# Relative-position attention: the score band moved in 64-row pieces, one band buffer for each tile, and the output stored tile by tile

## Chip, cores and metric

The kernel runs on one core of a Trainium2 chip. The metric is the device time of one execution in microseconds (us), the median of several runs. The engines are named as in the profile: PE (TensorE matmul) and PEld (its weight loads), DVE (VectorE), ACT (ScalarE), POOL (GpSimd) and SP (SyncE, which here only issues transfers). SPq and POOLq stand for the issuing side of SP and POOL.

## What is computed

The program is a two-layer network over 16 sequences of 256 positions with 128 features. Each layer normalises its input and adds an attention part and a mixture-of-experts part to the residual. The change lies in the attention of the second layer, which has 16 heads of 8 features and a learned vector for each clipped distance:

```
idx = jnp.arange(s)
dist = jnp.clip(idx[None, :] - idx[:, None], -R, R) + R      # R = 64
pe_k = rel_emb_k[dist]
pe_v = rel_emb_v[dist]
score = jnp.einsum('bhqd,bhkd->bhqk', q, k) + jnp.einsum('bhqd,qkd->bhqk', q, pe_k)
attn = jax.nn.softmax(score, axis=-1)
ctx = jnp.einsum('bhqk,bhkd->bhqd', attn, v) + jnp.einsum('bhqk,qkd->bhqd', attn, pe_v)
```

The second score term depends on key minus query, clipped at 64 to either side. A tile of 128 queries needs it on a band that runs along the diagonal; outside the band it is constant in a row, and the kernel subtracts that constant, so that the term is zero there.

## The kernel before

The stages follow one another in blocks, at whose end all engines meet: a first stage (normalisation and the first mixture), the first attention, the second mixture, the second attention (`attn1_stage`) and a last block that stores the output (`store_stage`, one transfer of 2 MB).

The second attention takes 32 tiles of 128 queries, two for each of 16 sequences. An even tile holds the first 128 queries of its sequence (`it` 0), an odd tile the last (`it` 1). Each engine has its own written-out order, `step(r, i)`, for tile `s = 4r + i`. A tile has 8 pairs of heads (`hp`), in four quarters of two pairs (`q`). While tile `s` is scored, the band of tile `s + 1` is made and moved, and the weighted values of tile `s - 1` are finished:

- PE multiplies queries by the distance table into `ps_R` (`rel_scores`, L1407) for tile `s + 1`. ACT copies that into `Rt` (`keep_R`, L1542).
- SP sends a quarter of `Rt` to DRAM (`send_band`, L1741), into rows of `PITCH` pairs of values, and reads it back with a row stride that is one pair shorter (`fetch_band`, L1750). So each row is moved by one more position than the row above, and what was indexed by distance is indexed by key. Beside the band the DRAM rows hold zeros, written in an earlier stage (`clear_dram`).
- DVE adds the fetched band `Sb` to the key scores and takes the row maximum (`add_scores`, L1609). ACT takes the exponentials, PE transposes them, and so on.

`Rt`, `Sb` and the two DRAM buffers `skew` are shared as follows: `skew` has one buffer for even and one for odd tiles; `Rt` and `Sb` are single. `Sb` is 320 keys wide, of which the band takes 192 and DVE clears 64 on either side once. Tile parity chooses which 256 of the 320 are read (`bias_of`).

The stacked operands of the next sequence (`stk`) also come by way of DRAM. POOL splits the projected queries and keys into three bf16 parts; SP writes the parts (`send_parts`, L1259) in an odd tile, reads nine query pieces in the next even tile (`stack_queries`, L1268, three in each of `fill(0)`, `fill(1)`, `fill(2)`) and three key pieces in the odd tile (`stack_keys`, L1278). PE needs all nine query pieces before the first `rel_scores` of the odd tile that follows.

SP issues in program order, and a wait holds all that is behind it:

```
fill(0)
send_band(s + 1, nit, 0)
fetch_band(s, it, 3)
fill(1)
send_band(s + 1, nit, 1)
fetch_band(s + 1, nit, 0)
fill(2)
send_band(s + 1, nit, 2)
fetch_band(s + 1, nit, 1)
```

After that come, in odd tiles, `send_parts`, and in all tiles `send_band` of quarter 3 and `fetch_band` of quarter 2. A send waits until ACT has copied its quarter (`R_ready`). A fetch waits until the send of its own quarter has landed (`skew_out`). ACT's copy of a quarter, and DVE's adding of it, wait until the fetch has landed (`skew_in`).

At the end of a tile's work DVE adds the two expert rows to it (`combine`, L1639), which finishes its 128 rows of `x_all`. POOL gathers those rows.

Of the kernel before, what the change touches and what calls it, by code (L numbers as in the profile page):

```python
# [12 lines left out]
P = 128  # L13
B, T, D = 16, 256, 128
# [961 lines left out]


ZW = 16
ZP = SLOTS // P * ZW // (2 * (P - 1))
CLEARS = D // ZW + 2 * 8 // ZP  # L980


def clear_dram(sp, zeros, slots_dram, skew, zeroed):

    for z in range(D // ZW):
        sp.dma_start(slots_dram.rearrange("(p s) d -> p s d", p=P)[:, :, z * ZW:(z + 1) * ZW],
                     zeros[:, :, :]).then_inc(zeroed, 16)
    some = zeros[:, :, :].rearrange("p a b -> p (a b)")[:, 0:ZP * 2 * (P - 1)].rearrange("p (n c) -> p n c", n=ZP)
    for p in range(0, HP, ZP):

        sp.dma_start(skew[0][:, p:p + ZP, 2 * BAND:2 * PITCH], some).then_inc(zeroed, 16)
        sp.dma_start(skew[1][:, p:p + ZP, 0:2 * (P - 1)], some).then_inc(zeroed, 16)
# [192 lines left out]
REL = 64  # L1185
NREL = 2 * REL + 1
BAND = P + REL
PITCH = BAND + P - 1
GI = 16
GH1 = GI // 2  # L1190
PARTS = 3
# [10 lines left out]
class Attn1Front:  # L1202


    def __init__(self, m):
        self.w_in = m.sb("a1w_in", [P, 3, D])
        self.w_out = m.sb("a1w_out", [P, D])
        self.qkf = m.sb("a1qkf", [P, 2, T])
        self.low = m.sb("a1low", [P, 2, T])
        self.prt = m.sb("a1prt", [P, PARTS, 2, T], BF16)  # L1210
        self.stk = [m.sb(f"a1stk{i}", [KS, 2, H1, T], BF16) for i in range(2)]
        names = ("loaded xb_ready qk_done qk_ready split parts_out stacked0 stacked1 v_done v_ready R_done R_ready "
                 "stacked_k0 stacked_k1 S_done S_ready P_ready T_done Ta_ready Tv_ready X_done X_ready c_done cT_ready rrep_ready "
                 "rdT_done rdT_ready y_done y_added pool_step vec_step cleared ids_ready rows_in first_added combined").split()
# [104 lines left out]
def attn1_stage(nc, front, x_all, xnT_all, a, gates, slot_ids, ident, one, bias_q, bias_k, bias_v, rel_st, tabs, pick, fold):  # L1319

    skew, parts = a["skew"], a["parts"]
    S2 = 2 * B
    LAG = 2
    RING = 4
    with Pool(nc) as m:
# [2 lines left out]

        vx = m.sb("a1vx", [P, 2, 2, H1, QW])
        Rt = m.sb("a1Rt", [P, HP, BAND, 2])
        Sb = m.sb("a1Sb", [P, HP, 2 * REL + BAND, 2])
        Pm = m.sb("a1Pm", [P, 2 * RING, T])
        nmx = [m.sb(f"a1nmx{i}", [P, H1]) for i in range(2)]
        PT = [m.sb(f"a1PT{i}", [P, 2, H1, P]) for i in range(2)]
# [36 lines left out]

            return h % (2 * RING)

        def bias_of(it, hp, n):

            c0 = REL * (1 - it)
            return Sb[:, hp, c0:c0 + T, n]

        def tiles_behind(r, i):

# [2 lines left out]
        with nc.Block() as block:  # L1385
# [150 lines left out]
            def _(act):  # L1536
                def keep_R(s, hp):
                    act.wait_ge(sm["R_done"], s * HP + hp + 1)
                    if hp % PQ == 0:

                        act.wait_ge(skew_in[hp // PQ], s * 16)
# [43 lines left out]
            def _(v):  # L1585
# [12 lines left out]
                def add_scores(r, i, hp):  # L1598

                    s = r * 4 + i  # L1600
                    it, par = tile_of(i)
                    if hp % PQ == 0:
                        v.wait_ge(skew_in[hp // PQ], (s + 1) * 16)
                    v.wait_ge(sm["S_done"], s * HP + hp + 1)
                    v.wait_ge(sm["T_done"], up(s * HP + hp + 1 - RING))
                    nc.vector.memset(taker[:, hp:hp + 1], 0.0)
                    for n in range(2):
                        h = 2 * hp + n
                        nc.vector.tensor_tensor_reduce(out=Pm[:, place(h), :], in0=ps_S[hp % 2][:, n, :], in1=bias_of(it, hp, n),  # L1609
                                                       scale=-1.0, scalar=3.0e38, op0=ALU.add, op1=ALU.min,  # L1610
                                                       accum_out=nmx[it][:, h:h + 1]).then_inc(sm["S_ready"], 1)

# [84 lines left out]
            @block.gpsimd  # L1697
            def _(pool):
                def copy_x(n):

                    pool.wait_ge(sm["v_done"], n)
                    nc.gpsimd.tensor_copy(xb[:, :], xnT_all[:, bass.ds(n * T, T)]).then_inc(sm["xb_ready"], 1)

                def gather(s):

                    pool.wait_ge(sm["combined"], s)
                    nc.gpsimd.tensor_copy(ids[:, :, :], slot_ids[:, :, bass.ds(s, 1)]).then_inc(sm["ids_ready"], 1)
                    pool.wait_ge(sm["ids_ready"], s + 1)
# [24 lines left out]

            @block.sync
            def _(sp):
                def send_band(s, it, q):

                    ps = slice(q * PQ, (q + 1) * PQ)
                    sp.wait_ge(sm["R_ready"], s * HP + (q + 1) * PQ)
                    c0 = 0 if it == 0 else 2 * (P - 1)  # L1740
                    sp.dma_start(skew[it][:, ps, c0:c0 + 2 * BAND], Rt[:, ps, :, :].rearrange("p n c h -> p n (c h)")).then_inc(skew_out[q], 16)  # L1741

                def fetch_band(s, it, q):

                    ps = slice(q * PQ, (q + 1) * PQ)
                    sp.wait_ge(skew_out[q], (s + 1) * 16)
                    flat = skew[it].rearrange("i n c -> (i n c)")
                    sp.dma_start(Sb[:, ps, REL:REL + BAND, :].rearrange("p n c h -> p n (c h)"),  # L1750
                                 bass.AP(flat.tensor, flat.offset + 2 * (q * PQ * PITCH + P - 1),
                                         [[2 * (HP * PITCH - 1), P], [2 * PITCH, PQ], [1, 2 * BAND]])).then_inc(skew_in[q], 16)

                def step(r, i):
                    s = r * 4 + i
# [37 lines left out]
                sp.wait_ge(keys_in[0], (B // 2 + 1) * KSTACK)  # L1793
                sp.wait_ge(sm["parts_out"], (B + 2) * 16)
                for q in range(QUARTERS - 1):
                    sp.wait_ge(skew_in[q], (2 * B + 1) * 16)
                sp.wait_ge(skew_out[3], (2 * B + 1) * 16)


def store_stage(nc, x_all, out):  # L1800
    with Pool(nc) as m:
        stored = m.sem("stored")
        with nc.Block() as block:
            @block.sync
            def _(sp):
                sp.dma_start(out.rearrange("b (t p) d -> p (b t) d", p=P), x_all[:, :, :]).then_inc(stored, 16)
                sp.wait_ge(stored, 16)


def program(nc, a):  # L1810
    with Pool(nc) as m:
# [73 lines left out]
```

## Time and profile before

| what | value |
|---|---|
| median of 3 runs | 1679.4 us (1679.25 to 1684.8) |
| profiled execution, first to last instruction (span) | 1677.5 us |
| PE / PEld / DVE / ACT / POOL busy over the span | 93% / 74% / 54% / 44% / 18% |
| second attention and output store | from 1102 us to the end |
| share of the 16 DMA engines, 1200 to 1600 us | 0.89, at 245 GB/s |
| granted PE clock, 1200 to 1600 us | 1.00 of 2.4 GHz |

The span is the one time that the trace has for the profiled execution; it lies 1.9 us under the median of the runs. Busy shares over the whole span are averages over stages with different limits, so the rows below are taken from the second attention alone. In a timeline row the bracket at the end gives the time for which the engine was idle before it, and what ended that time.

### The profile page before, as it was taken

How to read it: one execution, taken by the hardware profiler on the slowest of the kernel's cores; microseconds unless marked ns; L12 is line 12 of the kernel's file. 1: busy time of each engine (PE TensorE's matmuls, PEld its weight loads, DVE VectorE, ACT ScalarE, POOL GpSimd, SP SyncE). 2: the span in 40 equal slices, each digit the busy share in tenths (PEclk: the TensorE clock that was granted, in tenths of full speed). 3: DMA queues.
4: the chain of work that ended last, by engine and by line, in shares of the span. 5: the costliest groups of instructions: out<-in, count | busy, mean ns of one | idle time of the engine just before them, and what ended most of it. 6: DMA issues, size and time to landing. Idle time of an engine off the chain costs nothing. (4 is left out here: it accounts for less than half of the span.)

```text
span 1677.5 us, 38807 instructions
## 1 busy us (share of the span) xinstructions
PE 1552.2 (93%) x14424; PEld 1233.4 (74%) x14424; DVE 904.4 (54%) x3193; ACT 732.4 (44%) x1975; POOL 299.0 (18%) x376
## 2 busy tenths in 40 slices
PE   6899999999999999999599999959999999999996
PEld 5668888888888888888365656537777777777764
DVE  5336545454545454545322222237877777777774
ACT  2322222222222222222223232258888888888873
POOL 2010201111111101010430000003323332333232
PEclk9999999999999999999699999979999999999998
DMA  4009400000000000000243232258889998899886
GB/s 118 0 8 86 105 8 7 8 8 6 6 6 5 7 5 7 3 10 4 85 114 114 77 112 85 72 166 245 250 241 251 237 250 235 246 246 254 236 235 173
DMA packets 234032, 181.50 MB, mean 108 GB/s; under 512 B 82703, under 2 KB 223913, under 8 KB 233888
## 3 DMA queue, kind: packets, MB, share of 16 engines
q1 hardware_dynamic: 228514, 167.17, 37.1%
q0 software_dynamic: 5376, 12.44, 2.7%
q8 instruction: 89, 1.46, 0.4%
q14 instruction: 53, 0.43, 0.1%
HBM read 103.63 MB, written 75.78 MB: 107 GB/s over the span
## 5 line engine op out<-in xcount | busy, mean ns | idle before, releaser
L1547 ACT ACTIVATE a1Pm<-a1Pm,a1nmx 128x256 f32<-128x256 f32 x512 | 255.5, 504 | 0.4 <-DVE a1nmx L1609 0.3
L1609 DVE CUSTOM_DVE_ANT_0 a1Pm<-a1ps_S,a1Sb 128x256 f32<-128x256 f32 x512 | 196.1, 421 | 77.2 <-issue 75.5
L768 DVE TENSOR_TENSOR a0AT<-a0ps_AM,mask 128x384 f32<-128x384 f32 x256 | 125.5, 551 | 192.5 <-PE a0ps_AM L588 192.1
L773 DVE TENSOR_TENSOR a0MT<-a0ps_AM,mask 128x384 f32<-128x384 f32 x256 | 138.4, 555 | 88.2 <-PE a0ps_AM L609 85.1
L1542 ACT ACTIVATE a1Rt<-a1ps_R 128x384 f32<-128x384 f32 x264 | 128.6, 487 | 106.7 <-PE a1ps_R L1407 96.9
L1162 DVE TENSOR_TENSOR f1hid<-f1ge,f1ps_b 128x512 f32<-128x512 f32 x80 | 55.0, 688 | 192.1 <-PE f1ps_b L1095 182.4
L1426 PE MATMUL a1ps_T<-ident,a1Pm 128*128 128x128 f32 x1024 | 155.9, 275 | 0.0
L607 PE MATMUL a0ps_AM<-a0AT 128*128 128x256 f32 x512 | 152.9, 380 | 0.0
L572 PE MATMUL a0ps_qk<-xnT_all,a0w_in 128*128 (+1 forms) x512 | 138.3, 393 | 2.0 <-PEq L151 1.3
L715 ACT ACTIVATE a0qk<-a0ps_qk 128x512 f32<-128x512 f32 x128 | 76.4, 597 | 119.3 <-PE a0ps_qk L572 119.3
L1407 PE MATMUL a1ps_R<-rel_st,a1stk 72*128 72x192 bf16 x528 | 90.0, 253 | 35.5 <-ACT a1Rt L1542 13.2
L719 ACT ACTIVATE a0v<-a0ps_v 128x512 f32<-128x512 f32 x64 | 38.2, 597 | 191.0 <-PE a0ps_v L598 187.0
L1426 PEld LDWEIGHTS a1ps_T<-ident,a1Pm 128*128 128x128 f32 x1024 | 115.0, 142 | 0.4 <-issue 0.2
L723 ACT ACTIVATE a0oT<-a0ps_o 128x512 f32<-128x512 f32 x64 | 38.2, 597 | 170.2 <-PE a0ps_o L621 170.2
L608 PEld LDWEIGHTS a0ps_AM<-a0AT 128*128 128x128 f32 x512 | 97.3, 190 | 13.2
L1105 PE MATMUL f1ps_o<-f1wo,f1hid 128*128 128x128 f32 x768 | 90.0, 277 | 15.4 <-DVE f1hid L1162 15.4
L572 PEld LDWEIGHTS a0ps_qk<-xnT_all,a0w_in 128*128 128x128 f32 x512 | 87.1, 190 | 19.9 <-issue 12.1
L1105 PEld LDWEIGHTS f1ps_o<-f1wo,f1hid 128*128 128x128 f32 x768 | 87.0, 192 | 19.7 <-DVE f1hid L1162 11.9
L1416 PE MATMUL a1ps_S<-a1stk 72*128 72x256 bf16 x512 | 101.4, 280 | 0.0
L1093 PE MATMUL f1ps_a<-f1xT,f1w 128*128 128x512 f32 x192 | 100.0, 603 | 0.7 <-issue 0.7
L1547 ACT ACTIVATION_READ_ACCUMULATOR a1Pm<-a1Pm,a1nmx 128x1 f32 x512 | 99.6, 195 | 0.0
L609 PE MATMUL a0ps_AM<-a0AT 128*128 128x128 f32 x512 | 99.0, 275 | 0.0
(246 smaller groups left out, 2991.0 us busy)
## 6 DMA issues: line engine op xcount, KB each, us to landing
skew<-a1Rt SPq DMA_DIRECT2D x132, 384.0 KB, 5.4
a1Sb<-skew SPq DMA_DIRECT2D x131, 384.0 KB, 7.0
a1stk<-parts SPq DMA_DIRECT2D x153, 64.0 KB
a1stk<-parts SPq DMA_DIRECT2D x51, 192.0 KB
parts<-a1prt SPq DMA_DIRECT2D x18, 384.0 KB
f1w<-in_L_ffn_w_kernel SPq DMA_DIRECT2D x16, 344.0 KB
f1w<-in_L_ffn_w_kernel SPq DMA_DIRECT2D x16, 320.0 KB
f1wo<-in_L_ffn_wo_kernel SPq DMA_DIRECT2D x16, 320.0 KB
```

The source lines that it names most:

```text
L572: ins = nc.tensor.matmul(ps_qk[:, i, :], w_in[:, i, p * P:(p + 1) * P], xnT_all[:, bass.ds(b * T, T)], start=True, stop=True)
L607: nc.tensor.matmul(M[:, 0:T], S[:, 0:P], S[:, 0:T], start=True, stop=True)
L609: nc.tensor.matmul(M[:, T:HB], S[:, T:HB], S[:, T:HB], start=False, stop=True).then_inc(M_done, 1)
L768: nc.vector.tensor_tensor(AT[i][h][:, :], ps_AM[i][h][:, 0:HB], mask[:, :], ALU.mult).then_inc(A_ready, 1)
L773: nc.vector.tensor_tensor(MT[i][h][:, :], ps_AM[i][h][:, 0:HB], mask[:, :], ALU.mult).then_inc(M_ready, 1)
L1093: nc.tensor.matmul(ps_a[u % 2][:, :], w[i][:, u * P:(u + 1) * P], xT[i][:, :], start=True, stop=True).then_inc(a_done, 1)
L1105: ins = nc.tensor.matmul(ps_o[i][:, s, :], hid[:, c, s * P:(s + 1) * P], wo[i][:, c, :], start=(c == 0), stop=(c == HC - 1))
L1416: ins = nc.tensor.matmul(ps_S[hp % 2][:, n, :], stk[par][:, 0, h, it * P:(it + 1) * P], stk[par][:, 1, h, :], start=True, stop=True)
L1426: ins = nc.tensor.transpose(ps_T[k % 2][:, n, jt, :], Pm[:, place(2 * k + n), jt * P:(jt + 1) * P], ident[:, :])
L1542: nc.scalar.activation(Rt[:, hp, :, :], ps_R[:, :, :].rearrange("p n c -> p c n"), ACT.Copy).then_inc(sm["R_ready"], 1)
L1547: nc.scalar.activation(Pm[:, place(h), :], Pm[:, place(h), :], ACT.Exp, bias=nmx[it][:, h:h + 1], scale=-1.0, accum_out=den[it][:, h:h + 1 ...
L1609: nc.vector.tensor_tensor_reduce(out=Pm[:, place(h), :], in0=ps_S[hp % 2][:, n, :], in1=bias_of(it, hp, n), scale=-1.0, scalar=3.0e38, op0 ...
```

## The change

- A quarter of the band is sent as two transfers of 64 rows, and fetched as two. Each half moves only the columns that its rows need: for one half of the tile 128 pairs of values a row, for the other 192; it was 192 for all 128 rows. So there are 16 band transfers for each tile where there were 8, and a send or fetch of a quarter moves 128 KB and 192 KB in place of 384 KB. The semaphores of a quarter count 32 where they counted 16.
- `PITCH` goes from 319 to 320 pairs, so that a DRAM row is 2560 bytes long, not 2552; a sent row starts at a multiple of 512 bytes. The zeros beside the band are one pair wider.
- `Sb` becomes two buffers, one for even and one for odd tiles, each 256 keys wide. The part of each that no fetch writes is cleared once: that of the even buffer by DVE, that of the odd buffer by POOL (two clears each, over 64 rows). DVE waits for POOL's clears before its first step; SP and POOL no longer wait for DVE's.
- `store_stage` is gone. SP stores tile `s - 3` (64 KB) in the step of tile `s`, after the fetch of quarter 3 and before `fill(1)`, once `combine` has finished that tile. The last three tiles are stored after the last step, in the same block.

```diff
-PITCH = BAND + P - 1
+PITCH = BAND + P
...
-        Sb = m.sb("a1Sb", [P, HP, 2 * REL + BAND, 2])
+        Sb = [m.sb(f"a1Sb{i}", [P, HP, T, 2]) for i in range(2)]
...
+        def band_of(it, half):
+            keys = slice(0, P + half * REL) if it == 0 else slice(REL + half * REL, T)
+            return slice(half * REL, (half + 1) * REL), keys
...
-                nc.vector.memset(Sb[:, :, 0:REL, :], 0.0)
-                nc.vector.memset(Sb[:, :, REL + BAND:2 * REL + BAND, :], 0.0).then_inc(sm["cleared"], 1)
+                for half in range(2):
+                    ins = nc.vector.memset(outside(0, half), 0.0)
+                ins.then_inc(sm["cleared"], 1)
                 v.wait_ge(sm["cleared"], 1)
+                v.wait_ge(sm["edge_cleared"], 2)
...
-                pool.wait_ge(sm["cleared"], 1)
+                for half in range(2):
+                    nc.gpsimd.memset(outside(1, half), 0.0).then_inc(sm["edge_cleared"], 1)
+                    pool.wait_ge(sm["edge_cleared"], half + 1)
...
+                def store(s):
+                    sp.wait_ge(sm["combined"], s + 1)
+                    sp.dma_start(out_tiles[:, s, :], x_all[:, s, :]).then_inc(sm["stored"], 16)
...
-                    sp.dma_start(skew[it][:, ps, c0:c0 + 2 * BAND], Rt[:, ps, :, :].rearrange("p n c h -> p n (c h)")).then_inc(skew_out[q], 16)
+                    for half in range(2):
+                        rows = slice(half * REL, (half + 1) * REL)
+                        cols = slice((1 - half) * REL, BAND) if it == 0 else slice(0, BAND - half * REL)
+                        c0 = 2 * cols.start + (0 if it == 0 else 2 * P)
+                        wide = 2 * (cols.stop - cols.start)
+                        sp.dma_start(skew[it][rows, ps, c0:c0 + wide],
+                                     Rt[rows, ps, cols, :].rearrange("p n c h -> p n (c h)")).then_inc(skew_out[q], 16)
...
-                    sp.wait_ge(skew_out[q], (s + 1) * 16)
+                    sp.wait_ge(skew_out[q], (s + 1) * 32)
...
-                    sp.dma_start(Sb[:, ps, REL:REL + BAND, :].rearrange("p n c h -> p n (c h)"),
-                                 bass.AP(flat.tensor, flat.offset + 2 * (q * PQ * PITCH + P - 1),
-                                         [[2 * (HP * PITCH - 1), P], [2 * PITCH, PQ], [1, 2 * BAND]])).then_inc(skew_in[q], 16)
+                    for half in range(2):
+                        rows, keys = band_of(it, half)
+                        at = (P - 1 if it == 0 else P - REL) + keys.start - rows.start
+                        sp.dma_start(Sb[it][rows, ps, keys, :].rearrange("p n c h -> p n (c h)"),
+                                     bass.AP(flat.tensor, flat.offset + 2 * ((rows.start * HP + q * PQ) * PITCH + at),
+                                             [[2 * (HP * PITCH - 1), REL], [2 * PITCH, PQ], [1, 2 * (keys.stop - keys.start)]])).then_inc(skew_in[q], 16)
...
                     fetch_band(s, it, 3)
+                    if s >= 3:
+                        store(s - 3)
                     fill(1)
...
-                sp.wait_ge(sm["cleared"], 1)
...
+                for n in range(last - 2, last + 1):
+                    store(n)
+                sp.wait_ge(sm["stored"], 2 * B * 16)
...
-        store_stage(nc, x_all, a["out"])
```

## Rows read from the trace of the kernel before

**Rows 1.** Busy time of each engine in stretches of the second attention and store.

```profile
core 0: us, PE busy (x) PEld busy (x) DVE busy (x) ACT busy (x) POOL busy (x), PEclk, DMA share, GB/s
1200.00:1600.00 400.00, 382.73 (x5532) 300.55 (x5530) 307.88 (x1379) 332.27 (x1099) 124.40 (x167) 1.00 0.89 245
...
1666.00:1677.50 11.50, 0.00 (x0) 0.00 (x0) 0.00 (x0) 0.00 (x0) 0.00 (x0) 0.53 0.65 183
```

**Rows 2.** Timeline of PE: starts of tiles 9, 11 and 31, and two waits.

```profile
1262.06 0.38 PE L1416 MATMUL a1ps_S<-a1stk 72*128 72x256 bf16 x2
...
1295.43 0.39 PE L1416 MATMUL a1ps_S<-a1stk 72*128 72x256 bf16 x2
...
1298.06 1.13 PE L1225 MATMUL a1ps_p<-xnT_all,a1w_in 128*128 128x256 f32 x4 [0.73 <-DVE a1vx L1594]
...
1632.39 0.38 PE L1416 MATMUL a1ps_S<-a1stk 72*128 72x256 bf16 x2
...
1634.63 0.34 PE L1407 MATMUL a1ps_R<-rel_st,a1stk 72*128 72x192 bf16 x2 [1.86 <-DMA a1stk<-parts]
```

**Rows 3.** Chain of waits ahead of the late queries of tile 31: start us, us, what.

```profile
1605.13 8.99 DMA skew<-a1Rt
...
1614.61 6.26 DMA parts<-a1prt
...
1623.01 4.61 DMA skew<-a1Rt
...
1629.47 5.12 DMA a1stk<-parts
```

**Rows 4.** Timeline of SP's queue from the parts to the last queries of one even tile.

```profile
1242.22 0.54 SPq L1259 DMA_DIRECT2D parts<-a1prt  x1
...
1249.13 2.09 SPq L1268 DMA_DIRECT2D a1stk<-parts  x3
1251.26 0.45 SPq L1741 DMA_DIRECT2D skew<-a1Rt  x1
1251.76 0.48 SPq L1750 DMA_DIRECT2D a1Sb<-skew  x1
1252.29 2.39 SPq L1268 DMA_DIRECT2D a1stk<-parts  x3
...
1256.06 2.08 SPq L1268 DMA_DIRECT2D a1stk<-parts  x3
```

**Rows 5.** DMA view, 1200 to 1600 us: packets, then issues (count, KB, us to landing).

```profile
DMA packets 84263, 98.14 MB, mean 245 GB/s; under 512 B 5304, under 2 KB 81901, under 8 KB 84189
...
skew<-a1Rt SPq DMA_DIRECT2D x96, 384.0 KB, 6.4
a1Sb<-skew SPq DMA_DIRECT2D x96, 384.0 KB, 7.2
```

**Rows 6.** Landing of the stage's first band send, into an empty queue (1106 us).

```profile
DMA to landing us min/median/max: 2.5/2.5/2.5
```

**Rows 7.** Timeline of the start of the second attention.

```profile
1105.58 0.91 DVE L1682 MEMSET a1Sb<- 128x1024 f32 x1 [0.16 <-issue]
...
1106.52 4.75 SPq L1741 DMA_DIRECT2D skew<-a1Rt  x4
...
1111.31 1.65 SPq L1750 DMA_DIRECT2D a1Sb<-skew  x3
...
1115.67 0.49 ACT L1542 ACTIVATE a1Rt<-a1ps_R 128x384 f32<-128x384 f32 x1 [4.80 <-DMA a1Sb<-skew]
```

**Rows 8.** Timeline of the end: the last tile's last work, and the store.

```profile
1664.79 0.74 DVE L1639 SCALAR_TENSOR_TENSOR x_all<-a1rows,gates,x_all 128x128 f32<-128x128 f32 x2
1668.48 0.37 SPq L1806 DMA_DIRECT2D out<-x_all  x1
```

**Rows 9.** Landing of the output store.

```profile
DMA to landing us min/median/max: 8.7/8.7/8.7
```

**Rows 10.** A clear on POOL, from the groups of instructions with their shapes.

```profile
L189 POOL MEMSET mask<- 128x384 f32 x1 | 0.4, 417 | 0.0
```

More of the change, by code:

```diff
@@ L978 @@
 ZW = 16
-ZP = SLOTS // P * ZW // (2 * (P - 1))
+ZP = SLOTS // P * ZW // (2 * P)
 CLEARS = D // ZW + 2 * 8 // ZP
@@ L987, in clear_dram @@
                      zeros[:, :, :]).then_inc(zeroed, 16)
-    some = zeros[:, :, :].rearrange("p a b -> p (a b)")[:, 0:ZP * 2 * (P - 1)].rearrange("p (n c) -> p n c", n=ZP)
+    some = zeros[:, :, :].rearrange("p a b -> p (a b)")[:, 0:ZP * 2 * P].rearrange("p (n c) -> p n c", n=ZP)
     for p in range(0, HP, ZP):
         sp.dma_start(skew[0][:, p:p + ZP, 2 * BAND:2 * PITCH], some).then_inc(zeroed, 16)
-        sp.dma_start(skew[1][:, p:p + ZP, 0:2 * (P - 1)], some).then_inc(zeroed, 16)
+        sp.dma_start(skew[1][:, p:p + ZP, 0:2 * P], some).then_inc(zeroed, 16)
 def ffn1_stage(nc, w0_d, w1_d, wo_d, slots_dram, eo_dram, xn_all, send_ids, sent, ident, x_all, b_out, xnT_all, front, parts, one, bias_q, bias_k):
@@ L1213, in __init__ @@
                  "stacked_k0 stacked_k1 S_done S_ready P_ready T_done Ta_ready Tv_ready X_done X_ready c_done cT_ready rrep_ready "
-                 "rdT_done rdT_ready y_done y_added pool_step vec_step cleared ids_ready rows_in first_added combined").split()
+                 "stored rdT_done rdT_ready y_done y_added pool_step vec_step cleared edge_cleared ids_ready rows_in first_added combined").split()
         names += [f"skew_out{q}" for q in range(QUARTERS)]
@@ L1323, in attn1_stage @@
     skew, parts = a["skew"], a["parts"]
+    out_tiles = a["out"].rearrange("b (t p) d -> p (b t) d", p=P)
     S2 = 2 * B
@@ L1374, in place, with outside @@
             return h % (2 * RING)
-        def bias_of(it, hp, n):
-            c0 = REL * (1 - it)
-            return Sb[:, hp, c0:c0 + T, n]
+        def band_of(it, half):
+            keys = slice(0, P + half * REL) if it == 0 else slice(REL + half * REL, T)
+            return slice(half * REL, (half + 1) * REL), keys
+        def outside(it, half):
+            rows, keys = band_of(it, half)
+            return Sb[it][rows, :, keys.stop:T, :] if it == 0 else Sb[it][rows, :, 0:keys.start, :]
         def tiles_behind(r, i):
@@ L1539, in keep_R @@
                     if hp % PQ == 0:
-                        act.wait_ge(skew_in[hp // PQ], s * 16)
+                        act.wait_ge(skew_in[hp // PQ], s * 32)
                     nc.scalar.activation(Rt[:, hp, :, :], ps_R[:, :, :].rearrange("p n c -> p c n"), ACT.Copy).then_inc(sm["R_ready"], 1)
@@ L1602, in add_scores @@
                     if hp % PQ == 0:
-                        v.wait_ge(skew_in[hp // PQ], (s + 1) * 16)
+                        v.wait_ge(skew_in[hp // PQ], (s + 1) * 32)
                     v.wait_ge(sm["S_done"], s * HP + hp + 1)
@@ L1608, in add_scores @@
                         h = 2 * hp + n
-                        nc.vector.tensor_tensor_reduce(out=Pm[:, place(h), :], in0=ps_S[hp % 2][:, n, :], in1=bias_of(it, hp, n),
+                        nc.vector.tensor_tensor_reduce(out=Pm[:, place(h), :], in0=ps_S[hp % 2][:, n, :], in1=Sb[it][:, hp, :, n],
                                                        scale=-1.0, scalar=3.0e38, op0=ALU.add, op1=ALU.min,
@@ L1739, in send_band @@
                     sp.wait_ge(sm["R_ready"], s * HP + (q + 1) * PQ)
-                    c0 = 0 if it == 0 else 2 * (P - 1)
-                    sp.dma_start(skew[it][:, ps, c0:c0 + 2 * BAND], Rt[:, ps, :, :].rearrange("p n c h -> p n (c h)")).then_inc(skew_out[q], 16)
+                    for half in range(2):
[5 more added lines that the diff above has]
+                                     Rt[rows, ps, cols, :].rearrange("p n c h -> p n (c h)")).then_inc(skew_out[q], 16)
                 def fetch_band(s, it, q):
                     ps = slice(q * PQ, (q + 1) * PQ)
-                    sp.wait_ge(skew_out[q], (s + 1) * 16)
+                    sp.wait_ge(skew_out[q], (s + 1) * 32)
                     flat = skew[it].rearrange("i n c -> (i n c)")
-                    sp.dma_start(Sb[:, ps, REL:REL + BAND, :].rearrange("p n c h -> p n (c h)"),
-                                 bass.AP(flat.tensor, flat.offset + 2 * (q * PQ * PITCH + P - 1),
-                                         [[2 * (HP * PITCH - 1), P], [2 * PITCH, PQ], [1, 2 * BAND]])).then_inc(skew_in[q], 16)
+                    for half in range(2):
+                        rows, keys = band_of(it, half)
+                        at = (P - 1 if it == 0 else P - REL) + keys.start - rows.start
+                        sp.dma_start(Sb[it][rows, ps, keys, :].rearrange("p n c h -> p n (c h)"),
+                                     bass.AP(flat.tensor, flat.offset + 2 * ((rows.start * HP + q * PQ) * PITCH + at),
+                                             [[2 * (HP * PITCH - 1), REL], [2 * PITCH, PQ], [1, 2 * (keys.stop - keys.start)]])).then_inc(skew_in[q], 16)
                 def step(r, i):
@@ L1795, in _ @@
                 for q in range(QUARTERS - 1):
[L1796 to L1807, printed above, removed]
+                    sp.wait_ge(skew_in[q], (2 * B + 1) * 32)
+                sp.wait_ge(skew_out[3], (2 * B + 1) * 32)
+                for n in range(last - 2, last + 1):
+                    store(n)
+                sp.wait_ge(sm["stored"], 2 * B * 16)
 def program(nc, a):
```

## Prediction

> **What bounds the kernel now.** The change touches only the second attention and the store behind it, so I read those by stretches first [rows 1]. From 1200 to 1600 us PE is busy for 382.73 of 400 us at a granted clock of 1.00, its higher level, 2.4 GHz. DVE, ACT and POOL each have room. The DMA engines have little: a share of 0.89. In the last 11.5 us no compute engine is busy at all, and only DMA works.
>
> Then the timeline of PE [rows 2]. Tile 9 starts at 1262.06 and tile 11 at 1295.43: a pair of tiles takes 33.37 us. Tile 31 starts at 1632.39, eleven pairs after tile 9; eleven times 33.37 is 367.1, the trace has 370.3. So in all that stretch just 3.3 us go to disturbances. PE sets the pace, and the transfers mostly keep up.
>
> The chain of waits shows what a disturbance is [rows 3]. PE waits 1.86 us for tile 31's late queries [rows 2]. Behind that stand a band send that landed after 8.99 us, which held back a fetch and behind it the parts (6.26 us to land), the next band send (4.61 us, which held back a fetch and behind it the last queries) and the queries (5.12 us). A send of the same 384 KB into an empty queue lands after 2.5 us [rows 6], so most of this is queueing. The chain runs through SP's program order, which the change makes longer. That is the place to watch.
>
> Last, the end [rows 8, 9]. DVE's last work ends at 1664.79 + 0.74 = 1665.53 us. The store is issued at 1668.48, since a new block begins first, and lands 8.7 us later at about 1677.2; the span ends at 1677.5.
>
> The sum below is made against this span. The median of the runs is 1.9 us above it, and I carry that difference over unchanged. About 0.5%, 8.4 us, is what a measurement of this kernel can tell from no change; so "faster" means under 1671.0 and "slower" over 1687.8.
>
> **The end: −9.8 us.** Removed: a change of block (2.95 us between DVE's last work and the issue) and a store of 2 MB (8.7 us). Added at the same place: one store of 64 KB, whose wait DVE's last work ends. The other 31 are issued earlier; the two before it wait for work done at least 5 us before. No row has a 64 KB store by itself. From above it is bounded by the 2.5 us of a 384 KB send into an empty queue [rows 6]; from below by its issue plus its share of the big store, 0.37 + 8.7/32 = 0.64 us. I take 1.8, nearer to the send, because that too is one transfer from SBUF to DRAM into an empty queue. The end then comes at 1665.53 + 0.1 + 1.8 + 0.3 = 1667.7 in place of 1677.5. The bounds give −9.1 to −11.0.
>
> **Stores inside the stage: 0.** Each adds one issue on SP (0.37 us [rows 8]) and 64 KB of traffic. `combine` of tile s − 3 ends at the end of step s − 1 or just after, ahead of SP's place for the store, so SP shouldn't wait. The issue itself is counted in the chain below.
>
> **Band traffic.** Of the 98.14 MB in 400 us, 192 band transfers of 384 KB are 75.5 MB [rows 5], 77%. The change removes a sixth of them, 12.6 MB, and adds 1.6 MB of stores (24 tiles). That leaves 87.1 MB, 11% less; at the same cost per byte the DMA share falls from 0.89 to 0.79. Nobody waits for a mean share, so by itself this is worth nothing; it shortens landings.
>
> **Band issues.** SP issues 16 where it issued 8, 0.45 to 0.48 us each [rows 4]. In an even tile SP is packed from the parts' landing (1249.13) to the end of the last queries' issue (1258.14). Walked along the chain of rows 3: the second half of the send that gates the parts goes out 0.4 us later; the second half of the fetch ahead of the parts takes 0.4. After the parts' landing, SP needs two sends (0.90), two fetches (0.96), a store (0.37), three queries (2.39) and two sends (0.90), 5.5 us, before the next fetch, where before the landing of the send gated it (4.61 us): 0.9 later. That fetch has a second half too, 0.4. So the last queries are issued 2.1 us later, if landings stay as they are. Behind them on SP wait the sends of quarters 2 and 3, and for these ACT and DVE one tile later.
>
> Against this stand shorter landings and slack. PE waits 0.73 us for DVE's `a1vx` anyway before `project_qk` [rows 2], and queries up to that much later cost nothing. The landings on the chain exceed the 2.5 us of an empty queue by 6.5 (first send), 3.8 (parts) and 2.6 us (queries) in the bad tile, 12.9 in sum. An ordinary tile has 6.9 us from the parts' issue to the first queries [rows 4], 4.4 over. If the excess falls only with the bytes, by 11%, the bad chain gains 1.4 us; 2.1 − 1.4 = 0.7 is just covered by 0.73. If queueing at a share near 0.9 falls by more than the bytes, as I expect, there's a little to win. I take −1.0 us of the stage's 3.3 us of disturbances plus the 1.86 in tile 31. Bounds: −5.2 (all of it), and with no relief at all (2.1 − 0.73) × 15 odd tiles = +21.
>
> **The start: +0.8 us.** ACT waits 4.80 us for the first fetch, until 1115.67 [rows 7]. SP's sends no longer wait for DVE's clears (the last ends at 1106.49, the first send goes out at 1106.52), but the last of the four waits for ACT's last copy in any case. Ahead of the first fetch's landing now stand one more send and one more fetch issue, 0.8 us; the same again stands ahead of the first sequence's last queries. Fewer bytes and an earlier queue take some back: 0 to +1.6, I take +0.8.
>
> **Clears: 0.** DVE clears 2048 + 1024 elements a row in place of twice 1024 (0.91 us each [rows 7]), 0.9 us more, and then waits for the first fetch until about 1115.7. POOL's two clears are, at 417 ns for 384 elements [rows 10], about 3.3 us, and DVE's wait for them ends near 1106. With that cover of 8 us gone they'd cost 0.9 us on DVE.
>
> **Alignment and the second `Sb`: 0.** The fetch still shifts each row by 8 bytes. The sends become aligned; at 2.5 us for 384 KB with the old pitch they have little to give, and no row speaks for a loss. No fetch was ever issued later for want of a free `Sb`, and the new waits allow none earlier. DVE reads bands with the same step as before.
>
> Sum: −9.8 − 1.0 + 0.8 = −10.0 us: a span of 1667.5, a median of 1669.4 us.
>
> **Half of the partitions: a rival from a price no row has.** All large transfers in these rows use 128 rows; none shows what 64 rows cost. From below, the same per byte; from above, twice as much, if half of the rows reach half of the memory's ways in. I take the same, since rows 5 and 6 are the nearest, and because both halves, and sends beside fetches, are in flight together. In numbers for a pair of tiles: DMA works 0.89 × 33.37 = 29.7 us, 22.9 for the band and 6.8 for the rest. After the change 19.1 + 7.3. At a factor f per byte the DMA time passes 33.37 from f = 1.36, and the run gets slower than before by over 0.5% from about f = 1.43. At f = 1.5: 36.0 us a pair, 2.6 × 16 = +41, about 1711 us; at f = 2, +195.
>
> The Trainium skill speaks for this rival: SBUF — State Buffer, "Door 1: The DMA port swizzle", has a transfer of partitions 0 to 63 reach only half of the ports, 196 GB/s against 328 for 128 partitions at 1 MiB, and finds that two such halves issued together hardly gain. That would be f = 1.67 and, as an estimate from that page, 5.8 × 16 = +93 us, 1763 us. No run here shows it, and the measured 245 GB/s at a share of 0.89 mix many transfers.
>
> **Rivals and chances.**
> 1. The end is saved and the rest is hidden (forecast): 1666 to 1674, about 1669.4. Speaks for it: eleven pairs lose 3.3 us in all. 0.52, of which 0.12 end above 1671.
> 2. The relief is full, disturbances vanish too: 1664 to 1666. For it: 12.9 us of queueing in the bad chain; against it: the longer order on SP. 0.12.
> 3. SP's order becomes the bound: the last queries come late in each odd tile. With no relief +21 + 1.0, 1691; with half, about 1680. For it: SP is packed already [rows 4]. 0.18, of which 0.08 above 1687.8.
> 4. Half pieces move slower (above), 1690 to 1760. 0.15, nearly all slower.
> 5. The store of 64 KB or the end of the block takes as long as what it replaces: 1676 to 1680. Against it: no compute engine is busy in the last 11.5 us. 0.03.
>
> Faster 0.52, same 0.25, slower 0.23. The forecast's own range is 1666 to 1674. The range for 8 in 10 goes from 1664 (full relief) to 1692 (no relief), and leaves most of rival 4 out.
>
> **What would show it.** Right: the store of the last tile issues at once behind DVE's last work and lands in about 1.8 us; a pair of tiles still takes 33.37 us; DMA moves some 218 GB/s at a share near 0.79; PE's wait for `a1stk` stays under 1 us in most odd tiles. Wrong: a pair above 33.4 us with waits at `rel_scores` on `a1stk` of 1 us and more (rival 3), or a DMA share as high as before at fewer GB/s, with DVE and ACT waiting for `a1Sb` (rival 4).

## The result: 1702.85 us, slower by 1.4 %

The changed kernel takes 1702.85 us in the median of 4 runs (1700.61 to 1707.38), beside 1679.72 us for the kernel before on the same chip. The ratio is 1.0137, with a 95 % interval of 1.0111 to 1.0162. The forecast was 1669.4 us, and the time lies outside its range of 1666 to 1674 and above 1692, the end of its range for 8 in 10, on the side of rivals 3 and 4.

The first view is that of busy time by stretches, of the changed kernel; it answers to [rows 1]. The second row begins as DVE's last work ends. The last three numbers of a row are the granted clock of PE, the share of the DMA engines and their GB/s.

```profile
1200.00:1600.00 400.00, 367.44 (x5103) 289.15 (x5104) 288.15 (x1292) 309.17 (x1020) 115.97 (x155) 0.97 0.81 203
...
1698.90:1702.00 3.10, 0.00 (x0) 0.00 (x0) 0.04 (x1) 0.00 (x0) 0.00 (x0) 0.50 0.07 21
```

The DMA engines are less busy, 0.81 where it was 0.89, and yet PE is busy for 15 us less in the same 400 us. The DMA view of the same stretch (columns as in [rows 5]) shows that transfers land earlier too: 3.6 to 4.1 us after their issue, where it was 6.4 and 7.2.

```profile
DMA packets 84076, 81.01 MB, mean 203 GB/s; under 512 B 8144, under 2 KB 81861, under 8 KB 84005
...
a1Sb<-skew SPq DMA_DIRECT2D x90, 192.0 KB, 3.6
skew<-a1Rt SPq DMA_DIRECT2D x89, 192.0 KB, 4.1
```

So a higher load of the DMA engines isn't what holds PE up. PE's timeline (answering to [rows 2]) gives the place. Tile 9 starts at 1269.11 and tile 31 at 1667.42, 398.3 us for eleven pairs where it was 370.3.

```profile
1252.66 0.39 PE L1422 MATMUL a1ps_S<-a1stk 72*128 72x256 bf16 x2
...
1269.11 0.39 PE L1422 MATMUL a1ps_S<-a1stk 72*128 72x256 bf16 x2
...
1272.17 0.50 PE L1413 MATMUL a1ps_R<-rel_st,a1stk 72*128 72x192 bf16 x2 [2.68 <-DMA a1stk<-parts]
...
1290.92 0.28 PE L1422 MATMUL a1ps_S<-a1stk 72*128 72x256 bf16 x1
...
1667.42 0.38 PE L1422 MATMUL a1ps_S<-a1stk 72*128 72x256 bf16 x2
```

The even tile 8 still takes 16.45 us. The odd tile 9 takes 21.81, where an undisturbed one took 33.37 − 16.45 = 16.92, since PE waits 2.68 us for the query pieces at its first `rel_scores`. In this tile what comes behind the wait costs as much again. In the view by stretches the granted clock is 0.52 for 6.8 us from the end of the wait, the lower of its two levels (1.2 GHz), and 1.00 a little later:

```profile
1272.20:1279.00 6.80, 6.80 (x31) 5.84 (x33) 3.56 (x19) 5.10 (x17) 1.45 (x3) 0.52 0.90 235
1280.00:1290.00 10.00, 10.00 (x156) 7.74 (x159) 7.39 (x30) 7.03 (x24) 3.33 (x4) 1.00 0.94 193
```

Not every such wait is followed by this. Of the twelve between 1200 and 1600 us (0.30 to 3.85 us long) five have a stretch of 4 us with a mean clock under 0.95 behind them; the kernel before has no such stretch there. What it costs over all eleven pairs is seen in two more rows, from the start of tile 9 to that of tile 31, first before the change, then after:

```profile
1262.06:1632.39 370.33, 353.17 (x5084) 277.06 (x5082) 283.94 (x1276) 305.93 (x1011) 114.96 (x154) 1.00 0.89 243
...
1269.11:1667.42 398.31, 363.43 (x5085) 285.49 (x5082) 285.38 (x1276) 306.36 (x1011) 115.04 (x154) 0.97 0.81 202
```

PE does the same matmuls in both (5084 and 5085 records). Of the 28.0 us more, 10.3 are PE being busy for longer, at a mean clock of 0.97 in place of 1.00, and 17.7 are idle time.

Over the span the view of PE's waits (us in total, times, longest) shows this wait 15 times, almost once in each odd tile; before it was 6.4 us in 6 waits. The view of SP's waits shows the other side: SP now waits far less. Its fetches wait 37.5 us for sends to land and its sends 24.3 us for ACT, where it was 119.6 and 103.1.

```profile
PE a1ps_R L1413 <- DMA a1stk<-parts: 32.4, 15, 3.8
...
SPq L1770 <- DMA skew<-a1Rt: 37.5, 18, 3.7
...
SPq L1759 <- ACT a1Rt L1548: 24.3, 53, 1.5
```

The same rows of the kernel before:

```profile
PE a1ps_R L1407 <- DMA a1stk<-parts: 6.4, 6, 2.0
...
SPq L1750 <- DMA skew<-a1Rt: 119.6, 69, 6.3
...
SPq L1741 <- ACT a1Rt L1542: 103.1, 66, 3.8
```

The timeline of SP in the same even tile as in [rows 4], from the parts to the last queries:

```profile
1253.26 0.52 SPq L1259 DMA_DIRECT2D parts<-a1prt  x1
...
1256.99 2.13 SPq L1268 DMA_DIRECT2D a1stk<-parts  x3
1259.16 1.28 SPq L1759 DMA_DIRECT2D skew<-a1Rt  x2
1260.48 1.78 SPq L1770 DMA_DIRECT2D a1Sb<-skew  x2
1262.31 0.59 SPq L1748 DMA_DIRECT2D out<-x_all  x1
1262.94 2.13 SPq L1268 DMA_DIRECT2D a1stk<-parts  x3
1265.12 1.28 SPq L1759 DMA_DIRECT2D skew<-a1Rt  x2
1266.44 1.27 SPq L1770 DMA_DIRECT2D a1Sb<-skew  x2
```

Once the parts have landed, each row begins 0.04 to 0.05 us after the row above it has ended. SP goes from one issue to the next and no landing stops it. The last three query pieces follow at 1267.75 and are issued by 1269.87, when tile 9 has already begun. Measured from the start of tile 8, the parts go out at +0.60 (before −3.40, with this row of PE's timeline of the kernel before), and the last queries at +17.21 (before +12.52):

```profile
1245.62 0.39 PE L1416 MATMUL a1ps_S<-a1stk 72*128 72x256 bf16 x2
```

The 4.69 us between are 4.00 later for the parts, −3.18 for their landing (3.73 in place of 6.91) and +3.87 for SP's issues between that landing and the last queries (12.88 in place of 9.01).

The medians of one issue, by line (ns, min/median/max, in the views of single lines), are 0.61 us for a half send or fetch; a whole send had 0.38 and a whole fetch 0.37 (the last two rows, of the kernel before).

```profile
L1759 SPq DMA_DIRECT2D skew<-a1Rt x264: 574/612/2069, 1103.6 to 1686.4; - x132
...
L1770 SPq DMA_DIRECT2D a1Sb<-skew x262: 592/611/1922, 1111.3 to 1687.7; - x131
...
L1741 SPq DMA_DIRECT2D skew<-a1Rt x132: 359/382/1487, 1106.5 to 1651.6; - x132
...
L1750 SPq DMA_DIRECT2D a1Sb<-skew x131: 359/366/1732, 1111.3 to 1652.0; - x131
```

With 0.69, 0.43, 0.53 and 0.60 us for a query piece, a key piece, the parts and a store (medians of their lines), SP's queue for a pair of tiles holds 32 × 0.61 + 9 × 0.69 + 3 × 0.43 + 0.53 + 2 × 0.60 = 28.7 us, and 47 gaps of 0.04 make 30.6 of the 33.37 us that PE needs. Before it was 16 × 0.38 + 6.2 + 1.3 + 0.4 + 29 × 0.04 = 15.1. By this estimate from medians the queue is 92 % full without a single wait, and 2.8 us a pair are left. SP's waits that remain (37.5 + 24.3 us over 16 pairs, 3.9 a pair) don't fit into that.

The end answers to [rows 8]: DVE's last work, then the store of the last tile.

```profile
1698.20 0.74 DVE L1645 SCALAR_TENSOR_TENSOR x_all<-a1rows,gates,x_all 128x128 f32<-128x128 f32 x2 [2.07 <-DMA a1rows<-eo,a1ids]
1698.97 0.33 SPq L1748 DMA_DIRECT2D out<-x_all  x1
```

The span ends at 1702.0, 3.06 us behind DVE's last work; it was 11.97. All in all: +2.5 us up to the start of tile 2 (1147.87 in place of 1145.33), +4.5 to tile 9, +28.0 to tile 31, −1.6 in the last tile, −8.9 at the end, which makes the 24.5 us between the spans.

### The profile page after: what moved, and what is told of

The parts are those of the page before. It is cut to its first block and busy times, and to the rows that moved or that the text cites. A ratio compares the mean times of both kernels' runs of the same rounds, so it can differ in the third digit from the quotient of the medians.

```text
span 1702.0 us, 39083 instructions
## 1 busy us (share of the span) xinstructions
PE 1563.5 (92%) x14416; PEld 1245.1 (73%) x14424; DVE 905.9 (53%) x3193; ACT 733.2 (43%) x1975; POOL 302.0 (18%) x378
## 5 line engine op out<-in xcount | busy, mean ns | idle before, releaser
L1432 PE MATMUL a1ps_T<-ident,a1Pm 128*128 128x128 f32 x1024 | 163.0, 283 | 0.3 <-ACT a1Pm L1553 0.3
L1432 PEld LDWEIGHTS a1ps_T<-ident,a1Pm 128*128 128x128 f32 x1024 | 120.7, 147 | 0.9 <-ACT a1Pm L1553 0.6
L1413 PEld LDWEIGHTS a1ps_R<-rel_st,a1stk 72*128 72x128 bf16 x528 | 46.7, 101 | 88.5 <-ACT a1Rt L1548 38.4
```

The source lines that it names most:

```text
L1413: ins = nc.tensor.matmul(ps_R[:, n, :], stk[par][:, 0, 2 * hp + n, it * P:(it + 1) * P], rel_st[:, it, :], start=True, stop=True)
L1432: ins = nc.tensor.transpose(ps_T[k % 2][:, n, jt, :], Pm[:, place(2 * k + n), jt * P:(jt + 1) * P], ident[:, :])
```

## Experiments

Theory A: SP's time for issues is what holds the queries up. Theory B: half-partition transfers move more slowly, and that holds the band up. Ratios are to the kernel before, with 95 % intervals.

**The stores alone.** The kernel before with only the store changed.

```diff
+                    if s >= 3:
+                        store(s - 3)
...
-        store_stage(nc, x_all, a["out"])
```

> The kernel before, with the output stored tile by tile and nothing else of the change. Theory A (SP's issuing is the bound: the band pieces cost SP too much time in its program order): one issue of 0.4 to 0.6 us more a tile is mostly covered, the end is 9 us shorter; 1668 to 1674 us, and waits of PE for a1stk as before, under 1.2 us in most odd tiles. Theory B (64-row transfers move slower): says the same, 1671. Theory C (the stores inside the stage hold up the chain): 1685 us or more, with waits for a1stk in most odd tiles.

0.9962 [0.9941, 0.9982], some 6 us faster. The end gains as in the changed kernel (3.0 us behind DVE's last work), so about 3 us are lost inside the stage; PE waits 13.9 us for the queries in place of 6.4, most single waits under 1.3 us and the longest 2.7. A store is an issue of 0.71 us in the median, ahead of the last queries in SP's order.

**The price of an issue by its rows.** Behind the end of the kernel before, SP issues transfers one by one, each after the last has landed: two pairs of heads, 384 values a row, from 128, 64, 32, 16 and 8 rows. Then come sends and fetches in a row, as whole pieces and as halves. The kernel's own work is unchanged, and only what follows it is read here.

```diff
+                    for r0, rows in ((0, 128), (0, 64), (64, 64), (0, 32), (0, 16), (0, 8)):
+                        for again in range(2):
+                            sp.wait_ge(one_by_one, 16 * n)
+                            sp.dma_start(*form(0, r0, rows)).then_inc(one_by_one, 16)
```

> The kernel before with a block added at the end, whose only work is band-like transfers of 128, 64, 32, 16 and 8 rows, first one at a time and then several in a row; only these are read. Theory A: a 64-row issue takes 0.57 to 0.61 us on SP even in an empty queue, a 128-row issue 0.36 us, and 64 rows land no later than 128 rows. Theory B: the issue takes the same for both, and 192 KB in 64 rows land as late as 384 KB in 128 rows (2.5 us) or later.

The timeline of SP, sends of 128 (twice), 64, 64, 32, 16 and 8 rows; the start of the next one tells when a transfer had landed:

```profile
1675.36 0.37 SPq L1832 DMA_DIRECT2D skew<-x_all  x1
1677.86 0.36 SPq L1832 DMA_DIRECT2D skew<-x_all  x1
1680.35 0.67 SPq L1832 DMA_DIRECT2D skew<-x_all  x1
1683.11 0.60 SPq L1832 DMA_DIRECT2D skew<-x_all  x1
...
1691.15 0.33 SPq L1832 DMA_DIRECT2D skew<-x_all  x1
...
1694.76 0.30 SPq L1832 DMA_DIRECT2D skew<-x_all  x1
...
1698.28 0.28 SPq L1832 DMA_DIRECT2D skew<-x_all  x1
```

An issue of 64 rows costs more than one of 128: 0.60 to 0.67 us against 0.37. 32, 16 and 8 rows cost 0.33, 0.30 and 0.28. The price is thus no matter of size, and theory A was right on it. On the landing theory B was: 192 KB from 64 rows land as late (1680.35 to 1683.11, 2.76 us) as 384 KB from 128 rows (2.50). That isn't the time of moving alone, since the issue is 0.3 us longer and even 8 rows (24 KB) take 1.6 us from their issue to the next (1698.28 to 1699.9). In a row 1.5 MB take 7.4 us in whole pieces (1731.79 to 1739.20) and 8.4 us in halves (1739.20 to 1747.57). But SP's issues alone take 2.1 us of the first and 5.2 of the second, so this isn't proof that halves move more slowly. The share of the DMA engines, times the length, is nearly the same for both, 0.73 × 7.41 = 5.4 and 0.67 × 8.37 = 5.6 us:

```profile
1731.79:1739.20 7.41, 0.00 (x0) 0.00 (x0) 0.00 (x0) 0.00 (x0) 0.00 (x0) 0.50 0.73 212
1739.20:1747.57 8.37, 0.00 (x0) 0.00 (x0) 0.00 (x0) 0.00 (x0) 0.00 (x0) 0.50 0.67 188
```

The Trainium skill (DMA: Bandwidth & Descriptors, "Rules for kernel authors") says that two transfers to disjoint halves of the partitions gain nothing and that one transfer of 128 should be used; the rows here agree, as the halves in a row gained nothing over whole pieces (8.4 us against 7.4).

**Twice as many pieces, all of 128 rows.** The stores alone, and each quarter moved as two pieces of one pair of heads, at full width: the same bytes as before, the changed kernel's number of issues.

```diff
-                    ps = slice(q * PQ, (q + 1) * PQ)
+                    for hp in range(q * PQ, (q + 1) * PQ):
+                        ps = slice(hp, hp + 1)
```

> The kernel before with the stores tile by tile and each quarter of the band moved in two pieces of all 128 rows (one pair of heads each, full width): as many band issues as in the changed kernel, no 64-row piece. Theory A with the cost in the 64-row form: 0.37 to 0.45 us an issue, the chain 1 to 2 us longer, 1672 to 1685 us. Theory A with the cost in the count or the size of pieces: 0.6 us an issue and about 1700 us. Theory B: no 64-row pieces, so as with the stores alone, 1671 us.

1.009 [1.0058, 1.0121]. That is 1.3 % over the stores alone, from the count of pieces without any half-partition transfer, which speaks against theory B. PE waits 30.5 us in 14 waits for the queries. Of theory A neither form holds whole: an issue takes 0.43 to 0.45 us, as in the first, and the time is above the range that went with it. By the count of medians used in the section on the result, SP's queue holds some 24.5 us a pair here, 73 % of 33.37. So the queue needn't be nearly full for more issues to cost time.

**Halves at full width.** The changed kernel with 192 pairs a row in every half: its issues, the bytes of before.

```diff
-            keys = slice(0, P + half * REL) if it == 0 else slice(REL + half * REL, T)
+            keys = slice(0, BAND) if it == 0 else slice(REL, T)
...
-                        cols = slice((1 - half) * REL, BAND) if it == 0 else slice(0, BAND - half * REL)
+                        cols = slice(0, BAND)
```

> The changed kernel with its 64-row pieces at the full width of 192 pairs: the same issues, a fifth more band bytes. Theory A (SP's issuing is the bound): the bytes saved are worth little, 1.010 to 1.022 of the kernel before, as the changed kernel's 1.014. Theory B (the DMA engines are the bound): a fifth more bytes in slow pieces is felt in every pair of tiles, 1.030 or more.

1.0274 [1.0239, 1.0309]: slower than theory A said and not quite as slow as B. With the same issues the wider halves cost 1.35 % more, so theory A is not the whole. Landings are still part of the chain (send, fetch, parts, queries): SP waits 53.8 us for sends to land, where the changed kernel has 37.5, and ACT 31.6 us for fetches, where it has 23.8, up to 6.0 at a time. PE's waits for the queries grow to 48.9 us. In tile 8 the last queries are issued no later than in the changed kernel (+17.02 us from the tile's start, there +17.21), but PE goes on 3.49 us behind that issue, not 2.30.

**Room on SP.** The changed kernel with each tile's query parts written to DRAM three times (one write for each part), and read by 3 transfers in place of 9: more bytes, but 6 long issues less a pair of tiles for 3 more writes.

```diff
-            sp.dma_start(front.stk[par][c * PARTS * HD + k:(c + 1) * PARTS * HD:PARTS, 0, :, :],
-                         q_rows[:, (k + c) % PARTS, 0, :, :]).then_inc(front.queries_in[par], 16)
+        sp.dma_start(front.stk[par][c * PARTS * HD:(c + 1) * PARTS * HD, 0, :, :],
+                     parts[1][c].rearrange("(h d) k t -> (d k) h t", d=HD)).then_inc(front.queries_in[par], 16)
```

> The changed kernel with the query parts written to DRAM three times over, so that three transfers of 24 rows fetch the stacked queries where nine of 8 rows did: SP issues 3 more transfers before the parts land and 6 fewer behind them, and 0.39 MB more is written for each pair of tiles. Theory A: some 4 us come off SP's chain between the parts and the last queries; PE's waits for a1stk of 2 to 4 us go below 1 us; 1668 to 1678 us. Theory B: the DMA engines have more to do, not less; 1700 us or more.

0.9964 [0.9943, 0.9986], 1.7 % faster than the changed kernel, while the DMA share goes up to 0.89. Less work for SP and more for the DMA engines makes it faster. This speaks against theory B. The waits for the queries don't all go below 1 us, as expected: 18.4 us are left, in 11 waits, the longest of 3.7.

The rows are the share over 400 us, the start of tile 8 on PE, and the last query transfer on SP:

```profile
1200.00:1600.00 400.00, 374.39 (x5310) 294.82 (x5309) 296.83 (x1331) 319.75 (x1060) 122.75 (x163) 0.98 0.89 220
...
1249.22 0.39 PE L1424 MATMUL a1ps_S<-a1stk 72*128 72x256 bf16 x2
...
1260.81 0.56 SPq L1270 DMA_DIRECT2D a1stk<-parts_q  x1
```

The last queries are issued at +12.15 us from the start of tile 8, where the changed kernel has +17.21 and the kernel before +12.52. The queue as a whole shrinks by less: by the same count it holds 28.1 us a pair in place of 30.6. What shrank is mostly what stands ahead of the queries.

**The whole band with the same room.** The stores alone, and the three query transfers of the run above.

```diff
-QSTACK = 16 * PARTS * PARTS
+QSTACK = 16 * PARTS
...
+                    if s >= 3:
+                        store(s - 3)
```

> The kernel before with the stores tile by tile and the three-fold query parts (three transfers of 24 rows in place of nine of 8), the band in 128-row pieces as before. Theory A: SP's chain gets some 4 us shorter than in the kernel with the stores alone, so the late queries vanish; 0.988 to 0.994 of the kernel before, which would be faster than both. Theory B: 0.39 MB more for each pair of tiles at a DMA share of 0.88 makes it slower than the stores alone (0.996), 1.00 or more.

0.9924 [0.9896, 0.9951], at a DMA share of 0.95. Beside the 0.9964 of the halves, the narrower halves are no gain even where SP has room.

**The pieces alone.** The changed kernel with the old last block for the output in place of the stores.

```diff
-                    if s >= 3:
-                        store(s - 3)
...
+        store_stage(nc, x_all, a["out"])
```

> The changed kernel with the output stored as before, 2 MB at the end in a block of its own: the band pieces alone. Theory A: loses the 7 to 9 us of the shorter end and gains up to 2 for the issues that are gone; 1.016 to 1.020 of the kernel before. If the stores inside the stage did the harm (theory C): 1.005 or less.

1.0143 [1.0107, 1.018], as slow as the whole change (1.0137). That is less than expected, and speaks against theory C. The 9 us that the stores save at the end are given back inside the stage, within what the intervals allow. Each store is one more issue of 0.60 us in a packed queue, but how that comes to 9 us isn't shown: in the two profiled executions PE's idle time from 1102 us to DVE's last work is the same (some 62 us), and what differs is how long its same matmuls take, 525.46 us here and 535.22 with the stores, at a mean clock of 0.97 and 0.95.

**The store last in SP's step.** The whole band with three query transfers, and the store behind `fetch_band` of quarter 2.

```diff
-                    if s >= 3:
-                        store(s - 3)
                     fill(1)
...
                     fetch_band(s + 1, nit, 2)
+                    if s >= 3:
+                        store(s - 3)
```

> As the kernel with the stores and three query transfers, but SP stores a tile at the end of its step, behind the last band transfers, not between the first and the second query transfer. Theory A: one issue of 0.4 to 0.7 us less on the chain that brings the queries; as that kernel or up to 0.2% faster. Theory B: no difference.

0.9898 [0.9872, 0.9925], 1666.35 us: the best version here, faster than both kernels. It is 0.26 % ahead of the one with the store early, a little more than expected, though the two intervals overlap. In its views by stretches and of SP's waits, the DMA engines are busier than ever and SP waits again:

```profile
1200.00:1600.00 400.00, 381.21 (x5508) 299.36 (x5505) 307.47 (x1380) 331.41 (x1096) 123.89 (x167) 1.00 0.95 261
...
SPq L1757 <- DMA skew<-a1Rt: 136.7, 63, 4.7
```

**Issues with next to no bytes.** The stores alone, and behind each band transfer two transfers of 8 rows and 64 bytes a row, which nothing reads or waits for inside the stage. No band transfer is changed.

```diff
+                def two_small():
+                    for _ in range(2):
+                        n = next(small)
+                        sp.dma_start(a["small"][n], ident[0:8, 0:16]).then_inc(sm[f"small{n % 4}"], 16)
```

> The kernel before with stores tile by tile (band whole, 128 rows), and behind every band transfer two transfers of 8 rows and 64 bytes a row from the identity to a scratch tensor that nothing reads: sixteen more issues a tile, nearly no bytes, no wait on them inside the stage. Theory A (SP's issue time is the bound): at the 0.27 to 0.28 us that 8 rows took alone, 16 x 0.275 = 4.4 us more of SP's queue a tile, where the change adds 16 x 0.61 - 8 x 0.46 = 6.1; so a loss of about 4.4/6.1 of the 29 us between stores alone and the changed kernel, some 20 us: a ratio near 1.008, bounds 1.003 to 1.015, with SP's waits gone and PE waiting for the queries stack in most odd tiles. Theory B (what costs is how the half transfers move): the ratio of stores alone, 0.994 to 0.999, since no band transfer is changed.

1.0165 [1.0136, 1.0193]. Issues alone reproduce the loss. The band doesn't land later for them (sends after 4.9 us, fetches after 4.3, where the stores alone have 4.9 and 5.1), and the last queries are issued at +18.3 us from the start of tile 8. The trace looks like that of the changed kernel (stretches, PE's waits there, and the line of the small issues):

```profile
1200.00:1600.00 400.00, 364.58 (x5077) 285.75 (x5077) 283.36 (x1271) 305.91 (x1011) 113.77 (x151) 0.97 0.82 230
...
PE a1ps_R L1409 <- DMA a1stk<-parts: 24.1, 11, 4.1
...
L1747 SPq DMA_DIRECT2D small<-ident x526: 289/358/2528, 1104.4 to 1695.0; - x176
```

It is more than the 1.008 expected and above its bounds. The size was off because a small issue takes 0.36 us in this stage, not the 0.28 of the empty queue, and the whole-band sends beside it 0.46. Sixteen of 0.36 are 5.7 us a tile, near the 6.1 that the change adds.

**The halves with both helps.** The changed kernel with three query transfers and the store last.

```diff
                     fetch_band(s, it, 3)
-                    if s >= 3:
-                        store(s - 3)
...
                     fetch_band(s + 1, nit, 2)
+                    if s >= 3:
+                        store(s - 3)
```

> The changed kernel with its query parts written three times and queries fetched by 3 transfers in place of 9, and each tile's store as the last issue of SP's step. Theory A (SP's issue time is the bound): 0.6 us leave the chain between the parts and the last queries, 0.1 to 0.6 % faster than with the store early (0.9964): 0.990 to 0.996. Theory B (moving the halves is the bound): the order of a 64 KB store changes nothing, 0.995 to 0.998. If the narrow halves' smaller traffic is worth anything once SP has room, it would come out below the whole band with the same queries and store order (0.9898); I expect not.

0.9959 [0.9944, 0.9974]; with the store early it was 0.9964. Here the store's place can't be told from nothing, and both theories' ranges hold the value. The halves stay behind the whole band with the same order (0.9898, the intervals apart). What waits there is ACT, for the fetched band: 55.7 us in 30 waits, where the whole band has 13.4 in 6. Whether it comes late by SP's issues or by how halves move, no run separates.

## Why the prediction failed

**The step that failed is "Band issues".** It took 0.45 to 0.48 us for each of the 16 issues from rows of 128-row transfers, and walked one chain with it, from which it got +2.1 us, less relief. Two things were wrong. The form was new, and its issue takes 0.61 us: the stretch from the first send behind the parts' landing up to the gated fetch, which I put at 5.5 us, took 7.24 (1259.16 to 1266.40). And a chain in one tile doesn't show what the queue holds in all: 30.6 of 33.37 us a pair, by medians. SP came to the parts 4.0 us later, before the chain began. The last queries went out 4.7 us later in the tile shown, not 2.1, and the slack didn't cover it. The relief was there, as expected and more (landings −36 and −50 % in the DMA view), but it shortens waits of which SP has little left (37.5 us for landings of sends, where it was 119.6).

**Rival 3 was the right mechanism at too low a price.** Its worst case was +21 us; the span lost 33.4 before the end's gain. PE's waits for the queries grew by 26.0 us, and the price left out the lower clock behind them, 10.3 us over eleven pairs. PE's other waits nearly cancel: 9.4 us more for ACT's copy, 8.7 less for ACT's `a1PT` and 5.4 less for DVE's `a1vx`. Tile 9 is 4.89 us longer than the 16.92 it had, of which the wait, less the 0.73 us for `a1vx` that it covers, is 1.95.

**Rival 4 holds in part.** The DMA share was to be 0.79 and is 0.81, at 203 GB/s in place of 218. At 398.3 / 11 = 36.2 us a pair DMA works 0.81 × 36.2 = 29.3 us; less the 7.3 for the rest, the band takes 22.0 where 19.1 was forecast, a factor of 1.15. That is below the 1.36 from which DMA would have been the bound, and an estimate, as it takes the rest at the forecast's 7.3. The factor of 1.67 that the prediction estimated from the Trainium skill (SBUF — State Buffer, "Door 1: The DMA port swizzle") isn't reached with sends and fetches in flight together. The small issues show that issue time alone is enough for the whole loss (1.0165 without a half), and the three query transfers show that less to issue ahead of the queries takes it away at a higher DMA share; so rival 4 isn't the main cause. The halves at full width show that how the bytes move still counts. They move the same band bytes as the run with the small issues and lose 1.1 % more (1.0274 and 1.0165, the intervals apart). That may be the half-partition form, or the 1.8 us more that SP's queue holds for a pair by the same count (30.8 and 29.0); no run separates the two. Nor does any run move band issues to another engine's queue, which would test SP's time without touching a transfer's form.

**The end: right, −8.9 for −9.8.** The store lands after 1.5 us (1.8 was taken), but another 1.5 us lie between landing and the end of the span, where I had 0.3. (The term's lower bound works out at −10.9, not −11.0.)

**Stores inside the stage: wrong, not 0.** About 3 us where the band was moved whole, some 9, within the intervals, where SP is packed. The term left the issue to the chain, where it stood at 0.37 us; it is 0.60.

**The start: +2.5 for +0.8.** ACT's wait for the first fetch ended at 1115.42, 0.25 us earlier than before; the loss is in tile 1 (20.31 us in place of 17.53), with a wait of 2.77 us for its queries in place of 0.89, a wait of the same kind.

**Clears, alignment, second `Sb`:** nothing in the trace contradicts 0, but no run took them apart.

## What to carry over

Add up each queue's issues for one period of the kernel, with the duration of the form that will be used, before walking any chain. When the sum nears the period, shorter landings can't make up for it (here they fell by a third and more, and the kernel got slower); but with 73 % the cost is there too, so look at what stands ahead of the transfer that is waited for. Halving a transfer's rows to save a sixth of its bytes doubles the issues, and the queue's order turns every issue into delay for what stands behind it. Merging small transfers at the price of more bytes was the better trade here. That what nobody waits for (a store) belongs behind what somebody does is plausible but not shown: it was 0.26 % better once, with intervals that overlap, and no better the other time.

## Unexpected on the chip

- An issue of a 64-row transfer takes 0.57 to 0.67 us in an empty queue, more than 128 rows (0.36 to 0.38) and more than 32, 16 or 8 rows (0.33, 0.30, 0.28). Why isn't shown.
- Alone, 192 KB from 64 rows landed as late as 384 KB from 128 rows (2.76 and 2.50 us). In a row, the DMA engines were busy for nearly as long with halves as with whole pieces (5.6 and 5.4 us for 1.5 MB).
- In tile 9 the granted clock was 0.52 for 6.8 us behind a wait of 2.68 us of PE, so that the wait cost nearly twice its length. Behind seven of the twelve such waits in 400 us no stretch of 4 us shows it.
